# One NeuronCore, four GNN and four FFN layers: other arithmetic, buffers and bank counts in two segment-maximum passes, and another order of DMA issues beside one set of experts

## What is computed

```python
# L2: one score per edge, maximum over the edges of each SOURCE node
proj_s = feature @ W_s.T ; proj_t = feature @ W_t.T
z = proj_s[src] + proj_t[dst]
z = jnp.where(z >= 0, z, 0.2 * z)
e = (z @ W_attn.T)[:, 0]
m = jax.ops.segment_max(e, src, num_segments=n)
e_exp = jnp.exp(e - m[src]) ; denom = jax.ops.segment_sum(e_exp, src, n)
msg = feature[src] * (e_exp / denom[src])[:, None]
agg = jax.ops.segment_sum(msg, dst, num_segments=n) ; return agg @ W_fc.T + b_fc
# L3: four heads, maximum over the edges of each DESTINATION node
ft = (feat @ W.T).reshape(n, 4, 64)
e = jax.nn.leaky_relu(a1[src] + a2[dst], 0.2)
m = jax.ops.segment_max(e, dst, num_segments=n)
```

## Time and profile before

| | us |
|---|---|
| median of 3 runs | 6581.31 |
| lowest and highest | 6578.32, 6619.94 |
| profiled execution, its own time | 6642.85 |
| span of the profiled execution (first to last instruction) | 6641.0 |
| granted TensorE clock, mean of the span | 0.82 of full speed |

### The profile page before, as it was taken

The page is one execution under the profiler, slowest core; times in us unless marked ns, Lnnn a source line. Parts: engine busy times, 40 slices in busy tenths (PEclk is TensorE's granted clock), DMA queues, the critical chain, the costliest instruction groups (busy, mean ns, idle before and its releaser), DMA issues. The chain is left out here.

```text
span 6641.0 us, 91947 instructions
## 1 busy us (share of the span) xinstructions
PE 4618.0 (70%) x21663; PEld 2999.2 (45%) x21663; DVE 3846.8 (58%) x14461; ACT 2199.8 (33%) x7603; POOL 3545.6 (53%) x3819
## 2 busy tenths in 40 slices
PE   3556675838885555638667774787779488888868
PEld 3223233727772222424345553555568233336635
DVE  8676644131015666351568887777541677778875
ACT  0000000202232222302344444444323288874431
POOL 3736665556636666356556663666312366656630
PEclk9886656969996677755689997999879699989978
DMA  1133335646745666013155555778456166664410
GB/s 48 43 95 91 92 92 151 214 160 227 234 143 160 179 180 175 9 51 101 49 150 163 149 148 145 237 237 238 143 147 187 57 176 174 173 155 139 142 50 20
DMA packets 526131, 916.93 MB, mean 138 GB/s; under 512 B 100305, under 2 KB 382880, under 8 KB 517168
## 3 DMA queue, kind: packets, MB, share of 16 engines
q0 software_dynamic: 170800, 477.35, 26.4%
q1 hardware_dynamic: 294378, 305.07, 14.7%
q10 hardware_dynamic: 60438, 128.64, 6.2%
HBM read 739.33 MB, written 171.37 MB: 137 GB/s over the span
## 5 line engine op out<-in xcount | busy, mean ns | idle before, releaser
L1011 PE MATMUL bank<-small 128*125 128x256 f32 x1660 | 760.5, 580 | 474.2 <-DVE small L978 245.3
L959 POOL DMA_INDIRECT small<-tabA,idxD x830 | 809.8, 976 | 437.1 <-issue 192.0
L1011 PEld LDWEIGHTS bank<-small 128*125 128x125 f32 x1660 | 357.0, 263 | 876.7 <-issue 468.3
L990 DVE TENSOR_TENSOR big<-big,bank 125x256 f32 x830 | 347.4, 419 | 487.1 <-PE bank L1011 304.5
L2590 POOL DMA_INDIRECT small<-tabC,idxD x415 | 393.9, 949 | 323.5 <-issue 120.0
L2632 ACT ACTIVATE small<-cst,small 128x128 f32<-128x128 f32 x1660 | 531.5, 388 | 92.0 <-issue 35.3
L2643 PE MATMUL bank<-small 128*125 128x512 f32 x830 | 470.5, 651 | 128.4 <-issue 106.6
L2356 POOL DMA_INDIRECT big<-tabB,idxD x415 | 393.4, 948 | 300.4 <-PE bank L2419 146.4
L2170 POOL DMA_INDIRECT small<-tabT,idxS x415 | 395.4, 953 | 265.0 <-PE bank L2068 147.3
L1376 DVE COPY small<-bank 128x256 f32<-128x256 f32 x176 | 74.7, 425 | 796.4 <-PE bank L1431 467.7
L793 POOL DMA_INDIRECT recs<-pkS,rowS x391 | 383.9, 982 | 272.7 <-issue 102.9
(11 more groups left out here) (468 smaller groups left out, 11366.5 us busy)
## 6 DMA issues: line engine op xcount, KB each, us to landing
small<-eaS SPq DMA_DIRECT2D x830, 128.0 KB
big<-in_L_w ACTq DMA_DIRECT2D x56, 1024.0 KB
eaS<-small SPq DMA_DIRECT2D x415, 128.0 KB
big<-in_L2f_w ACTq DMA_DIRECT2D x64, 512.0 KB
ytab<-small ACTq DMA_DIRECT2D x176, 128.0 KB
big<-rowsS SPq DMA_DIRECT2D x52, 256.0 KB
small<-rowsD SPq DMA_DIRECT2D x52, 256.0 KB
small<-tabA,idxD POOLq DMA_INDIRECT x830
```

Source lines behind the costliest of these rows:

```text
L959: g.indirect_dma_start(out=self.gb[k % self.RG], out_offset=None, in_=K.tabA, in_offset=row_index(K.idxD, k)).then_inc(*self.got.up(k))
L990: v.tensor_tensor(rows, rows, K.bank[k % 4][0:PT, 0:D], ALU.add).then_inc(*self.added.up)
L1011: p.matmul(self.K.bank[k % 4][0:PT, 0:D], self.oh[k % self.RO][:, 0:PT], self.gb[k % self.RG], start=True, stop=True).then_inc(*self.summe ...
```

## The change

Every part of it, in words:

- **L3Max.** 16 gather buffers, a gather may be issued at most 12 tiles ahead of a finished field (AHEAD), 12 diagonal buffers (RD), 8 PSUM banks instead of 4. ACT makes two of the four diagonals (and still copies the scores), DVE the other two in one `tensor_tensor` of 256 columns. The one-hots per tile are gone: the diagonals are multiplied by a matrix of ones, and the mask is (identity - 1) * 1e30 times a transposed one-hot of 8 tiles at a time, which DVE makes from a row of `rowsD` that SP loads (256 KB, spread over the partitions). PE's two matmuls keep their size and kinds, but the mask comes first.
- **L2Max.** `tabT` has rows of 257 float32 instead of three bfloat16 parts. Tiles go in pairs through a bank (identity times both rows, 512 columns, then one one-hot matmul of 256 columns for each, all float32), 4 banks for sums; the field goes in groups of four tiles through 4 further banks. Per four tiles DVE makes one addition, one diagonal product of 512 columns, one maximum of 512 columns and one negation; ACT copies the linear parts and takes the four exponentials. 16 gather buffers. The transposed one-hots are float32, with 4 buffers.
- **L2Project.** The whole float32 projections are kept and stored beside the parts that `tabB` needs; `tabB` is stored here, not in L2Max. DVE makes one score product per window instead of two, and clears a buffer of 2316 columns at the start. One more small DVE instruction at the end.
- **L3Project.** Four scalings of the identity become one matrix and one column of lane numbers.
- **Experts of the first feed-forward layer.** The gather and two edge scatters, then a wait, then one edge scatter and the two record scatters.

```diff
@@ Moe.expert_gpsimd
             if k >= self.RX:
                 g.wait_ge(*self.e_flip.n(k - self.RX + 1))
+            if self.shared and k >= 4:
+                g.wait_ge(*self.e_hid[1].n(k - 3))
             g.indirect_dma_start(out=self.xg[k % self.RX], out_offset=None, in_=K.tabA, in_offset=row_index(self.tix, k)).then_inc(*self.rows_in.up(k))
-            if self.side and k >= 2:
+            if self.shared and k >= 2:
+                self.side.edges.gpsimd(g, 2)
+                if k >= 6:
+                    g.wait_ge(*self.e_y.n(k - 5))
+                self.side.edges.gpsimd(g, 1)
+                self.side.source.gpsimd(g, 2)
+            elif self.side and k >= 2:
                 self.side.gpsimd(g, 1)
@@ L2Project
+        v.memset(self.psB, 0.0).then_inc(*self.cleared.up)
...
-                for m in range(2):
...
-                    v.scalar_tensor_tensor(out=self.jk2[0:PT, :], in0=o[:, 0:D], scalar=0.2, in1=self.wat[0:PT, :], op0=ALU.mult, op1=ALU.mult,
-                                           accum_out=o[:, D:DL]).then_inc(*self.score.up)
+                v.scalar_tensor_tensor(out=self.jk2[0:PT, :], in0=o[:, 0:D], scalar=0.2, in1=self.wat[0:PT, :], op0=ALU.mult, op1=ALU.mult,
+                                       accum_out=o[:, D:DL]).then_inc(*self.score.up)
@@ L2Max
+    NZ, NF, RB, RD, LF, LR, LE = 4, 4, 16, 4, 2, 3, 4
...
     def gpsimd(self, g):
         for k in range(NTE):
-            if k >= 8:
-                g.wait_ge(*self.z.n(k - 7))
+            if k >= self.RB:
+                g.wait_ge(*self.z.n((k - self.RB) // 2 + 1))
+                g.wait_ge(*self.line.n((k - self.RB) // 4 + 1))
...
     def tensor(self, p):
+        for q in range(NP):
+            k, n = 2 * q, min(2, NTE - 2 * q)
...
+            p.matmul(z[:, 0:n * D].rearrange("p (t d) -> p t d", d=D), K.ident, self.rows(k, n)[:, :, 0:D], start=True, stop=False)
+            for i in range(n):
+                m = p.matmul(z[:, i * D:(i + 1) * D], flip.at(k + i)[0:PT, :], pr.ps[0:PT, bass.ds(offs[i], D)], start=False, stop=(i == n - 1))
+            m.then_inc(*self.z.up)
+            if (q % 2 == 1 or q == NP - 1) and q // 2 >= self.LF:
+                self.lay(p, q // 2 - self.LF)
@@ L3Max
-    RG = 8
+    RG, RD, BANKS, AHEAD, BUFS = 16, 12, 8, 12, 3
...
     def gpsimd(self, g):
             if k >= self.RG:
                 g.wait_ge(*self.kept_rows.n(k - self.RG))
                 g.wait_ge(*self.spread.n(k - self.RG + 1))
+                g.wait_ge(*self.half.n(k - self.RG + 1))
+            if k >= self.AHEAD:
+                g.wait_ge(*self.field.n(k - self.AHEAD + 1))
...
     def vector(self, v):
+                v.wait_ge(*self.got.n(i))
+                if i >= self.RD:
+                    v.wait_ge(*self.field.n(i - self.RD + 1))
+                v.tensor_tensor(self.diagonals(i, 2, 2).rearrange("p (h e) -> p h e", h=2), K.ident.unsqueeze(1).broadcast_to([128, 2, 128]),
+                                self.gb[i % self.RG][:, D + 2:D + 4].unsqueeze(2).broadcast_to([128, 2, 128]), ALU.mult).then_inc(*self.half.up)
...
     def scalar(self, a):
-            for h in range(4):
-                a.activation(self.dg[k % 4][:, h * 128:(h + 1) * 128], K.ident, ACT.Copy, scale=gb[:, D + h:D + h + 1])
+            for h in range(2):
+                a.activation(self.diagonals(k, h, 1), K.ident, ACT.Copy, scale=gb[:, D + h:D + h + 1])
...
     def tensor(self, p):
-            p.matmul(b[0:PT, :], self.oh[k % 4][:, 0:PT], self.dg[k % 4], start=True, stop=False)
-            p.matmul(b[0:PT, :], self.no[k % 4][:, 0:PT], pr.bigI4, start=False, stop=True).then_inc(*self.field.up)
+            p.matmul(b.rearrange("p (h e) -> p h e", h=4), pr.outside[:, 0:PT], inside.unsqueeze(1).broadcast_to([128, 4, 128]), start=True, stop=False)
+            p.wait_ge(*self.spread.n(k + 1))
+            p.wait_ge(*self.half.n(k + 1))
+            p.matmul(b, K.ones[:, 0:PT], self.dg[k % self.RD], start=False, stop=True).then_inc(*self.field.up)
```

More of the change, by code:

```diff
@@ L1958, in __init__, with whole, rest, third @@
         super().__init__(K, 2 * T)
-        self.prj = [g(DL) for _ in range(10)]
-        self.score, self.less = K.mark(2 * T), [K.mark(2 * T), K.mark(2 * T)]
+        self.rem = [g(DL) for _ in range(10)]
+        self.score, self.less = K.mark(T), [K.mark(2 * T), K.mark(2 * T)]
         self.part = [K.mark(2 * T) for _ in range(3)]
-        self.got, self.tab = K.dma(), K.ring(4, T)
-    def parts(self, t, i):
-        return self.prj[2 * (t % 5) + i][0:PT, :], (self.ps, self.pt)[i][0:PT, t * 2 * DP:t * 2 * DP + 3 * DL]
+        self.cleared = K.mark(1)
+        self.got, self.tabT, self.tabB = K.dma(), K.ring(self.RT, T), K.ring(self.RS, T)
+    def whole(self, t, m):
+        if m == 0:
+            return self.ps[0:PT, t * D:(t + 1) * D]
+        return self.ptF[0:PT, t % self.RT * DL:(t % self.RT + 1) * DL]
+    def rest(self, t, m):
+        return self.rem[2 * (t % 5) + m][0:PT, 0:(D, DL)[m]]
+    def third(self, t, m, c):
+        if m == 0:
+            at = t % self.RS * 2 * DP + c * DL
+            return self.psB.bitcast(BF16)[0:PT, at:at + D]
+        at = t * 2 * DP + c * DL
+        return self.pt[0:PT, at:at + DL]
     def gpsimd(self, g):
@@ new lines, in vector @@
+        for k in range(NTE):
+            v.wait_ge(*self.z.n(k // 2 + 1))
+            if k >= 2:
+                v.wait_ge(*self.score.n(k - 1))
+            v.scalar_tensor_tensor(out=self.jk[k % 2], in0=K.bank[k // 2 % self.NZ][:, k % 2 * D:(k % 2 + 1) * D], scalar=0.0, in1=pr.wat8,
+                                   op0=ALU.max, op1=ALU.mult, accum_out=pr.Ecol[:, k:k + 1]).then_inc(*self.score.up)
+            if k % 4 == 3 or k == NTE - 1:
+                g = k // 4
+                n = self.size(g)
+                four = slice(4 * g, 4 * g + n)
+                v.wait_ge(*self.line.n(g + 1))
+                v.wait_ge(*self.score.n(k + 1))
+                v.tensor_tensor(pr.Ecol[:, four], pr.Ecol[:, four], self.lin[:, four], ALU.add).then_inc(*self.whole.up)
+                if g >= self.LR:
+                    self.highest(v, g - self.LR)
+                if g >= self.RD:
+                    v.wait_ge(*self.field.n(g - self.RD + 1))
+                v.wait_ge(*self.whole.n(g + 1))
+                v.tensor_tensor(self.dg[g % self.RD][:, 0:n * 128].rearrange("p (t e) -> p t e", e=128), K.ident.unsqueeze(1).broadcast_to([128, n, 128]),
+                                pr.Ecol[:, four].unsqueeze(2).broadcast_to([128, n, 128]), ALU.mult).then_inc(*self.spread.up)
+                if g >= self.LR:
+                    self.lowered(v, g - self.LR)
+            if k % flip.G == 0 and k // flip.G + 2 < flip.n_g:
+                g = k // flip.G + 2
+                if g >= flip.BUFS:
+                    v.wait_ge(*self.field.n(2 * (g - flip.BUFS) + 2))
+                flip.vector(v, g)
@@ L2218, in tensor, with lay @@
+    def lay(self, p, g):
+        K, n = self.K, self.size(g) * 128
+        b = K.bank[self.NZ + g % self.NF]
+        if g >= self.NF:
+            p.wait_ge(*self.expo.n(4 * (g - self.NF) + 4))
+        p.matmul(b[0:PT, 0:n], self.pr.outside[:, 0:PT], self.flip.halves(4 * g, self.size(g)), start=True, stop=False)
+        p.wait_ge(*self.spread.n(g + 1))
+        p.matmul(b[0:PT, 0:n], K.ones[:, 0:PT], self.dg[g % self.RD][:, 0:n], start=False, stop=True).then_inc(*self.field.up)
     def tensor(self, p):
-        K, pr, LF, flip = self.K, self.pr, self.LF, self.flip
@@ L2242 @@
+        for g in range(NG - self.LF, NG):
+            self.lay(p, g)
 class L2Combine:
```

304 lines of the change are left out of this document (173 added, 131 removed).

## The result

Before 6579.82 us, after 6561.56 us (medians of ten runs each); ratio 0.9949, with a 95% interval from 0.9928 to 0.997. The forecast was 6380, 3.0% faster, with a range from 6285 to 6530: the time lies outside it. The gain is real and about a tenth of the forecast one; by the prediction's bound of 1% it counts as "no change".

What follows compares the result with a forecast made beforehand. It took POOL's 1.25 us per gather plus pauses between runs, from late news, as the bound in L2Max and L3Max. Terms -96 - 98 + 3 - 10 = -201 gave 6442 profiled, 6380 on the median's scale, range 6285 to 6530.

Steps and rivals of the forecast that it cites:

- bound of 1%: Whole kernel: a measurement tells about 1% (66 us) from no change.
- Cover: L3Max: 12 tiles of lead instead of 8 (15 us, not 10) and 8 banks cover the 2.2 us pause.
- rarer news of PE: L2Max: fewer matmul records may bunch PE's news every 6.4 tiles, 8 us of gathers, inside the cover.
- is told late: Gather stages: a done sum is told mostly 1 to 5 us late while POOL issues gathers, then several at once.
- 1.48 per tile for L1Sum: L1Sum, 613/415, with runs of 12 to 13: a warning that longer runs have pauses too.
- Rival B: News stays the limit, buffers hide nothing: L3Max 1.53 per tile, L2Max 1.44, total about 6525; chance 0.14.
- L3Max: -96: L3Max at 1.29 us per tile, 547 us in all; bounds 0 and -112.
- L2Max: -98: L2Max at 1.32 us per tile, 562 us in all; bounds -127 and -48.
- L2Project +3: L2Project: ACT bounds it, dropped score product worth 0, clearing costs 3.8 at most; bounds +4 and -10.
- Experts -10: First layer's experts: splitting POOL's six DMAs into runs of three gains 10 us; bounds -60 and +13.
- nothing in the change moves it: Gather stages: POOL's floor of 1.25 us per gather, 519 us for 415, stays the same.
- rival F: Each new DVE product waits for POOL, 0.36 us per tile; L3Max 626, total about 6460; chance 0.06.

Runs made afterwards that it cites:

- e16: Changed kernel with a lead of 20 instead of 12, 20 gather buffers and 4 transposed one-hots, on a chip with pauses: L3Max's gathers 617.6 us.
- e12: The changed kernel, unchanged, on a chip with pauses: whole time 6537.79 us in one run, L3Max's gathers 620 us.
- e14: Changed kernel with L3Max stripped to POOL's gathers, SP's stores and ACT's small copy, on a chip with pauses: L3Max's gathers 558.0 us.
- e3: Changed kernel with a lead of 8 tiles instead of 12, on a chip without pauses: L3Max's gathers 537.8 us.
- e11: The kernel before, unchanged, on a chip with pauses: whole time 6607.47 us in one run, L3Max's gathers 626 us.
- e1: Changed kernel with L3Max stripped to POOL's gathers and ACT's small copy, on a chip without pauses: L3Max's gathers 517.5 us.
- e17: Changed kernel with 28 waits instead of one ahead of each SP store in L3Max, on a chip without pauses: L3Max 541.5 us.
- e8: Changed kernel without the matmul that lays the mask in L3Max, on a chip without pauses: L3Max 534.6 us.

## Why the prediction failed

**The step that failed** is "Cover" in the part on L3Max, "The 2.2 us pause is less than the 5 us added", and the one like it for L2Max ("Cover goes from 8 buffers, freed one by one, to 16, freed by fours"). It took the pause for a delay that buffers outlast, and left 0.04 us per tile for it, 17 us in all. L3Max still has 84 us of it, and L2Max 71. A lead of 20 instead of 12 took some 2 us off (e16 against e12, whose chips agree within 1 us on the kernel before). Nor do the pauses go by matmul records, as the prediction has it for L2Max ("rarer news of PE"): e14 has them with no matmul in the stage. Nor does the size of the ring set how far apart the pauses lie: in the kernel before, L1Sum, L2Max and L3Max all have rings of 8, and their pauses over 1 us lie mostly 12, 3 and 7 or 8 gathers apart. The warning stood in the prediction: L1Sum with a pause every 12 to 13 gathers. I called its rings big; its ring is 8 (`EdgeSum`, RG), and that should have cast doubt on the cover as the reason.

The reading behind it, that a finished sum "is told late" and then several at once, came from the trace's semaphore updates. The trace of the kernel before holds 46,697 of them for 91,947 instructions, that of e3 111,652 for 84,733. By that measure more than half are missing from the first, and bunches of updates there show nothing about when the news came. The prediction's 1.48 per tile for L1Sum is a slip of another kind: it also counts what follows the last gather, and the gathers alone take 1.44.

Rival B had nearly the right price for L3Max (1.53; measured 1.498) and for L2Max (1.44; 1.458) and its total of 6525 was 37 us off. That is its price and not its reason: that the news is what limits was not shown. It got 0.14, for its only "against" was the releaser that the profile named.

**Term by term.** L3Max: -96 forecast, -12 measured in the profile: 30 us less of pauses, 18 more in longer gathers. DVE's product (0.42 to 0.43) and ACT (321 us busy) came as forecast. PE did not: it was put at 1.07 us per tile in L3Max and 1.13 in L2Max, from rows at full clock, and is busy 514/415 = 1.24 in both, at a granted clock of 0.90 and 0.94. That is still under the 1.50 and 1.46 that a tile takes. On chips without pauses the variants took 534 to 538 us from first to last gather, 1.29 to 1.30 each, which is the forecast 1.29; but there the kernel before has no pauses to lose. L2Max: -98 forecast, -43 measured: 58 us less of pauses, 13 more in longer gathers. That comes near its lower bound (-48). The change there is a bundle (buffers, fewer PE records, groups of four, shorter rows), and no run takes it apart, so what made this largest gain is not shown. L2Project +3: 705.0 before and 699.4 after in e11 and e12, 703 and 707 in the first pair; nothing clear of the noise. Experts -10: -17 to -20 in the pairs, and not in the pace beside the scatters, where it was expected, but behind them. L3Project 0: from L2Sum's last gather to L3Max's first 599, 607 and 602 us before, 609, 606 and 600 after, nothing clear of the noise.

**A term that was put at nothing.** The prediction has 1.25 us per gather as the floor "and nothing in the change moves it". But POOL's gathers themselves became longer. Groups of the changed kernel, beside L2590 at 949 and L2170 at 0.94 to 0.95 before:

```profile
L2703 POOL DMA_INDIRECT small<-tabC,idxD x415 | 412.3, 993 | 296.5 <-issue 97.3
L2247 POOL DMA_INDIRECT big<-tabT,idxS x415 | 408.8, 985 | 209.9 <-issue 111.5
```

and the place where it happens, L3Max of the changed kernel:

```profile
5501.11 0.42 DVE L2743 TENSOR_TENSOR big<-cst,small 128x256 f32<-128x256 f32 x1
5501.13 1.22 POOL L2703 DMA_INDIRECT small<-tabC,idxD  x1 [0.30 <-PE bank L2781]
```

The 91 gathers of L3Max that start while this product of DVE runs take 1.116 us on average, the other 324 take 0.959. In L2Max it is 1.312 (30 gathers, during the product of 512 columns) against 0.960. A gather that starts during a reduction from PSUM shows nothing of the kind (0.959). In L2Max DVE's transposed one-hot (L2197, one tensor in SBUF and a number per partition) does it too: the 40 gathers that run beside one and beside no product take 1.074, the 257 beside neither 0.946. Against the kernel before it is 18 us of POOL's time in L3Max and 13 in L2Max. The stripped loops, without DVE's work, have no gather over 0.962. This is the prediction's rival F, from the other side: not DVE waits for POOL, which the prediction rightly ruled out by the equal 421 and 419, but POOL for DVE. A hint was in the trace before: L959, in the stage that has L983, takes 976 ns against 948 to 949 for L2356 and L2590; but its gathers beside no L983 take 969, so most of that has another reason. The Trainium skill ("SBUF — State Buffer", section "SBUF: two separate sides") says as much, that a VectorE operation with two SBUF inputs takes the shared port pair against a GpSimd operation that reads SBUF; the runs agree in this direction. In the other they show no block: DVE's product takes 0.42 on average, whether a gather runs or not.

On a chip without pauses POOL's own pace bounds the stage, and there the longer gathers weigh fully: L3Max takes 1.299 us per tile in e3 with gathers of 0.992, and 1.250 with 0.945 when stripped (e1), on the same chip. Against the gathers of the kernel before (0.949 and 0.953, from chips with pauses) e3's 0.992 and 1.004 come to 18 us in L3Max and 21 in L2Max. With the 6 to 9 us behind L2Max, which were measured on chips with pauses, that is 45 to 48, within the 40 to 70 us by which the variants exceed the kernel before. That sum is worked out, not shown by a run.

**What else was lost.** Behind L2Max, 6 to 9 us: DVE takes maxima three groups and ACT exponentials four groups of four tiles late, so the last gather is followed by 16 tiles' work instead of four; that this is the reason is read from the code, no run tries another. L2Sum, 2 to 9 us: same instructions, but the granted clock falls from 0.98 to 0.92 and PE's busy time rises from 508 to 522 us (e11, e12; the other two pairs have 0.98 and 0.91 as well):

```profile
4049.00:4683.00 634.00, 508.21 (x3296) 349.02 (x3296) 472.53 (x2103) 285.04 (x820) 394.78 (x415) 0.98 0.81 238
```

```profile
3973.00:4616.00 643.00, 522.41 (x3307) 381.98 (x3308) 478.97 (x2112) 286.08 (x824) 393.23 (x415) 0.92 0.80 235
```

What PE did before differs, L2Max at 0.94 instead of 0.97; no run isolates it.

**What stays open.** What makes the pauses on some chips. Over the stages of e11, e12 and e14 the interval rises with the instructions per tile of all engines: 3.9 give 1.348 us, 10.3 give 1.426, 13.9 give 1.437, 18.8 give 1.457, 22.6 give 1.512 (L3Max before), 22.8 give 1.498 (after), 32.8 give 1.517 to 1.539, 36.7 give 1.545. That would explain why L2Max gained (36.7 to 18.8) and L3Max did not (22.6 to 22.8). It is a correlation over eleven stages. The run made to test it (e17) met a chip without pauses, and a kernel with fewer instructions in L3Max (e8) was tried only there too. The only such run on a chip with pauses, e14, strips nearly everything.

One rival stands beside all of this, and no run tests it: every time here comes with a span and a granted clock taken from records of the same execution. On the chips with pauses these records lack 60% of the semaphore updates that they hold elsewhere, and the pauses grow with the number of instructions. So it may be the recording that pauses the engines there, and not the kernel. A time taken without any recording would tell.

## What to carry over

When an engine pauses and all that it waits for has ended, compare stages before adding buffers: here three stages with a ring of 8 paused every 12, 3 and 7 or 8 gathers, so the ring didn't set it. Measure the floor alone (gathers only) and on more than one chip, because a gain that consists of removed pauses is worth nothing where there are none. Count the semaphore updates of a trace against its instructions before reading anything from when they come. And when DVE gets work on SBUF operands beside a stream of gathers, look at the gathers' durations, not only at DVE's.

## What the runs showed of the hardware

- Chips differ by 10% for the same program: the kernel before takes 5887 to 5919 us on three visits to two chips and 6580 to 6660 on four other visits. All runs of a visit were of one kind, and the one chip known to be met twice was of the same kind both times. The difference lies in the gather stages and the experts (after the change L1Sum 527 to 531 against 595 to 605 us, experts' first gather to L1Sum 529 to 549 against 589 to 594), while parts with few gathers agree (L2Sum to L3Max 601 to 610 against 599 to 609).
- On the chips with pauses the trace lacks 60% of the semaphore updates that it holds elsewhere (e12 45,489, e3 111,652, with as many instructions). In L3Max of the changed kernel, and hardly anywhere else, DVE's semaphore and register instructions take 0.70 us instead of 0.02 to 0.06 for 6 to 7 us at a time there, while those of ACT, POOL and PE keep their 0.02 to 0.05.
- A gather issued by POOL while DVE multiplies two SBUF operands takes 1.116 us on average (256 columns) or 1.312 (512 columns) instead of 0.96; one beside a float32 one-hot of 1024 columns takes 1.074 instead of 0.946. DVE's product keeps its 0.42 us.
